# A post-norm transformer layer on one core: the first unit's row maxima sent in two halves

## The chip, the cores and the metric

The kernel runs on one core of one Trainium2 chip. TensorE (PE in the profile) multiplies, VectorE (DVE) and ScalarE (ACT) read and write PSUM and SBUF, GpSimd (POOL) works in SBUF, SyncE (SP) issues nearly all DMAs. The time is the device time of one execution in microseconds; lower is better.

## The reference

Input `x` is 4 batches of 1024 tokens with 128 features, all float32.

```
q, k, v = x @ w_q, x @ w_k, x @ w_v              # 16 heads of 64
logits  = q k^T / 8, causal mask, softmax over keys
x = layernorm(x + (probs @ v) @ w_o^T)
h = butterfly_up(x @ W_exp + b_exp)              # 512 wide, 9 stages
h = butterfly_down(gelu(h + up_bias))            # 9 stages
x = layernorm(x + h @ W_con + b_con + down_bias)
```

## The kernel before

Attention is cut into 32 units: one batch and one pair of heads each. A unit has 12 steps. A step is one block of 128 keys (`kt`) against one chunk of 512 queries (`qc`): steps 0 to 3 are chunk 0, steps 4 to 11 chunk 1; on a diagonal block only the part at or right of the diagonal is computed. For each of the two heads a step has two score matmuls into a PSUM bank `SC`: L692 (keys by the high part of the queries) and L696 (keys by the low part). The projections are split into a part rounded to float32r (`QH`, `KHL`'s high half, made by ScalarE, L797) and the remainder (`QL`, made by VectorE, L929). ScalarE then takes the exponential (L863), GpSimd masks (L504) and adds the blocks up (L519, L527, L528), and the value matmuls (L717, `pv`) follow several steps later.

The softmax needs a row maximum for each query. It is found ahead of the unit with matmuls of its own (L631, "max" work) into one of four PSUM banks `WORK`; VectorE reduces each to a column of `MP` (L991 with the causal mask, an instruction and its accumulator read, or L994 without it). A unit has 21 such groups, `MAXES`: the first 6 (`CHUNK0_MAXES`) concern the queries of chunk 0, the other 15 those of chunk 1. At the last one VectorE forms the negated maxima `NEGM` (L998), transposes them to `NROW` (four instructions, L1004), and SyncE sends them as one row into partition 64 of `QL` (`rows`, L408), where L696 adds them to the scores. L696 of a unit's first step waits for it (`m_landed`).

All 21 groups of the coming unit, its four projections (`("proj", n, c)`: n is 0 for queries and 1 for keys, c the chunk) and its value projections (`("v", i)`) are spread as "fillers" over the 12 steps of the running unit, by the table `FILL`: three places for each step, between the two heads, behind the second, and after the step's value matmuls. TensorE executes in this written order. Each filler takes the next `WORK` bank and waits until the fourth filler before it has been emptied (`take_work`); VectorE and ScalarE empty them in the same order. `("proj", 0, 0)` is made one unit further ahead than the rest.

Unit 0 has no unit in front of it, so its fillers stand in a list of their own, `PREFETCH`, executed before the first step: two query and two key projections, two value projections, all 21 max groups, and the first projection of unit 1. While it runs, SyncE works through a fixed queue: the weights, the copies of queries and keys to the other half of the partitions (`copies(0)`, L396 and L400), the loads of `w_o`, `W_con` and two bias rows, a small copy of the bias row (L429) which GpSimd awaits before its last two bias stages (L190 to L494), `W_exp`, the second batch of `x`, and then `rows(0)`. GpSimd executes in written order too: the bias stages come before the first mask of unit 0. VectorE also splits the weights for coming units (`stage_low`, `stage_v_low`, L929 with the outputs `WST` and `WSV`): these read two SBUF tensors, whereas its reads of `WORK` take one from PSUM.

After 32 units come the feed-forward part and the last normalisation.

Of the kernel before, what the change touches and what calls it, by code (L numbers as in the profile page):

```python
# [194 lines left out]
def post_norm_layer(nc, x, w_q, w_k, w_v, w_o, W_exp, b_exp, up_w, up_b, down_w, W_con, b_con, down_b, out):  # L195
    ctx = ExitStack()
    with ctx:
# [161 lines left out]
        def _(sp):  # L359
# [72 lines left out]
            rows(0)  # L432
# [144 lines left out]
        def _(pe):  # L577
# [105 lines left out]
            def scores(unit, s):  # L683
# [3 lines left out]
                for h in range(2):  # L687
# [6 lines left out]
                    if s == 0 and h == 0:  # L694
                        pe.wait_ge(m_landed, (unit + 1) * 16)
# [223 lines left out]
        def _(dve):  # L919
# [40 lines left out]
            def consume(u, f, at):  # L960
# [19 lines left out]
                elif f[0] == "max":  # L980
                    pieces = f[1]
# [206 lines left out]
```

## Time and profile before

| | us |
|---|---|
| median of 3 runs | 1035.09 |
| lowest, highest | 1034.93, 1035.8 |
| the profiled execution | 1035.9 |
| its span, first to last instruction | 1034.2 |
| TensorE busy | 1007.0 (97%) |
| VectorE busy | 778.0 (75%) |
| GpSimd busy | 750.9 (73%) |
| ScalarE busy | 613.1 (59%) |
| mean granted TensorE clock | 0.993 of full |

The span leaves out 1.7 us of the profiled execution that lie around it. Busy shares are means over the whole program; the change touches only the first 60 us or so, and there the timeline and the stretches tell more. The chain that ended last runs 92% over TensorE. In the first of 40 slices TensorE is busy 6 tenths, in the second 7, in the third 9; from there to the end 9 in every slice, down to the last (7). A row that joins several instructions ("x2") gives their common start and total.

### The profile page before, as it was taken

Reading aid. Unit: us, or ns where it says so; the run is one execution under the profiler, and the core shown is the slowest. Engines: PE = TensorE matmul, PEld = TensorE weight load, DVE = VectorE, ACT = ScalarE, POOL = GpSimd, SP = SyncE. Lnnn points to the kernel's source line nnn. Section 1 sums busy time; section 2 is a strip of 40 time slices with the busy share of each in tenths; the row PEclk is TensorE's granted clock in tenths of the full one; section 3 lists DMA queues with packets and bytes.
Section 4 is the critical chain, followed back from the end, with each engine's and each line's share of the span. In section 5 each row is a group of like instructions: output and inputs, shape, how many; then the busy total and the mean of one; then the engine's idle time right before and its main releaser. Section 6 shows DMA issues by size and latency. Waiting matters only on the chain.

```text
span 1034.2 us, 17742 instructions
## 1 busy us (share of the span) xinstructions
PE 1007.0 (97%) x5816; PEld 697.7 (67%) x5816; DVE 778.0 (75%) x2112; ACT 613.1 (59%) x1246; POOL 750.9 (73%) x715
## 2 busy tenths in 40 slices
PE   6799999999999999999999999999999999999997
PEld 4566676676666776676666766767666766765687
DVE  7767777877777777878788778877778888785356
ACT  3555656566656656666556656666555656665544
POOL 6567887777768887777778877777778887777510
PEclk8899999999999999999999999999999999999999
DMA  6233122233222222232232222332222222320002
GB/s 190 62 83 82 45 72 53 62 83 83 58 68 62 63 65 60 63 83 63 70 76 58 62 56 55 83 83 63 66 60 74 63 57 57 83 64 22 22 11 73
DMA packets 48602, 68.71 MB, mean 66 GB/s; under 512 B 15191, under 2 KB 25083, under 8 KB 48510
## 3 DMA queue, kind: packets, MB, share of 16 engines
q1 hardware_dynamic: 48510, 67.57, 25.3%
q8 instruction: 47, 0.77, 0.3%
q14 instruction: 45, 0.37, 0.1%
HBM read 31.11 MB, written 2.36 MB: 32 GB/s over the span
## 4 chain that ended last, share of the span: by engine, by line
PE 92%; DVE 3%; DMA 2%; ACT 1%; issue 1%; POOL 0%; SPq 0%; POOLq 0%; ACTq 0%
PE O L717 25%; PE WORK L631 14%; PE SC L692 14%; PE SC L696 13%; PE WORK L644 6%; PE WORK L679 3%; PE WORK L607 3%; PE WORK L609 3%; PE WORK L608 3%; PE WORK L772 2%; PE WORK L617 1%; PE WORK L619 1%; PE WORK L618 1%; DVE WORK L991 1%; DMA R<-RROW 1%
## 5 line engine op out<-in xcount | busy, mean ns | idle before, releaser
L863 ACT ACTIVATE PR<-SC 128x512 f32<-128x512 f32 (+3 forms) x768 | 352.3, 490 | 263.9 <-PE SC L696 231.4
L519 POOL TENSOR_TENSOR SUM<-SUM,PR 128x1024 f32<-128x1024 f32 (+3 forms) x256 | 419.0, 1637 | 14.8 <-POOL SUM L528 0.5
L991 DVE CUSTOM_DVE_ANT_0 WORK<-WORK,CMASK 128x128 f32<-128x128 f32 (+3 forms) x512 | 239.3, 514 | 65.7 <-PE WORK L631 65.6
L692 PE MATMUL SC<-QH,KHL 128*128 128x512 f32 (+3 forms) x768 | 268.8, 356 | 3.1 <-ACT PR L863 3.0
L696 PE MATMUL SC<-QL,KH 128*128 128x512 f32 (+3 forms) x768 | 261.7, 346 | 3.3 <-DMA QL<-NROW 3.3
L504 POOL TENSOR_SCALAR_AFFINE_SELECT PR<-PR 128x256 f32<-128x256 f32 x256 | 105.9, 415 | 198.0 <-ACT PR L863 197.9
L631 PE MATMUL WORK<-KHL,QH 128*128 128x512 f32 (+3 forms) x768 | 226.5, 365 | 5.9 <-DMA KH<-KHL 4.1
L717 PE MATMUL O<-PR,VLO 128*64 128x512 f32 (+3 forms) x1024 | 200.0, 522 | 0.3 <-DVE OT L1075 0.3
L692 PEld LDWEIGHTS SC<-QH,KHL 128*128 128x128 f32 x768 | 145.2, 189 | 60.7 <-ACT PR L863 28.5
L631 PEld LDWEIGHTS WORK<-KHL,QH 128*128 128x128 f32 x768 | 136.7, 191 | 59.3 <-issue 35.4
L994 DVE TENSOR_REDUCE MP<-WORK 128x1 f32<-128x512 f32 x256 | 164.1, 684 | 4.8
L696 PEld LDWEIGHTS SC<-QL,KH 128*128 128x128 f32 x768 | 145.4, 189 | 14.2 <-DMA QL<-NROW 3.7
L929 DVE TENSOR_TENSOR QL<-WORK,QH 64x512 fp32r<-64x512 f32 x128 | 88.0, 687 | 86.7 <-ACT QH L797 85.5
L528 POOL TENSOR_TENSOR SUM<-PR 128x768 f32<-128x768 f32 x64 | 135.9, 2124 | 1.4 <-ACT PR L863 1.4
L717 PEld LDWEIGHTS O<-PR,VLO 128*64 128x64 f32 x1024 | 64.9, 136 | 104.4 <-issue 77.0
L929 DVE TENSOR_TENSOR KHL<-WORK,KHL 64x512 fp32r<-64x512 f32 x128 | 88.1, 689 | 34.2 <-ACT KHL L797 32.1
L797 ACT ACTIVATE QH<-WORK 64x512 fp32r<-64x512 f32 (+1 forms) x132 | 78.0, 591 | 26.2 <-PE WORK L609 22.6
L797 ACT ACTIVATE KHL<-WORK 64x512 fp32r<-64x512 f32 x128 | 75.7, 592 | 5.0 <-PE WORK L609 1.4
L717 PE MATMUL O<-PR,VHI 128*64 128x256 f32 (+3 forms) x512 | 74.3, 432 | 0.0
L991 DVE DVE_READ_ACCUMULATOR2_ANT MP<- 128x1 f32 x512 | 72.3, 141 | 0.0
L717 PEld LDWEIGHTS O<-PR,VHI 128*64 128x64 f32 x512 | 36.8, 137 | 52.6 <-issue 46.6
L644 PE MATMUL WORK<-WOT,OT 128*128 128x128 f32 x512 | 63.8, 278 | 0.6 <-DVE OT L1075 0.6
(132 smaller groups left out, 1099.0 us busy)
## 6 DMA issues: line engine op xcount, KB each, us to landing
QH<-QH SPq DMA_DIRECT2D x128, 128.0 KB, 2.4
KH<-KHL SPq DMA_DIRECT2D x128, 128.0 KB, 2.3
R<-RROW SPq DMA_DIRECT2D x64, 256.0 KB, 3.8
SW<-in_L_ffn_up_weights_dram SPq DMA_DIRECT2D x9, 512.0 KB, 4.4
SW<-_L_ffn_down_weights_dram SPq DMA_DIRECT2D x9, 512.0 KB, 4.3
out_dram<-X SPq DMA_DIRECT2D x7, 256.0 KB, 2.3
X<-in_L_attn_x_BSE_dram SPq DMA_DIRECT2D x3, 512.0 KB, 4.5
X<-in_L_attn_x_BSE_dram SPq DMA_DIRECT2D x2, 256.0 KB, 3.3
```

Of the source, the lines that this page charges most:

```text
L519: nc.gpsimd.tensor_tensor(total, total, prob(unit, s), ALU.add).then_inc(add_done, 1)
L528: nc.gpsimd.tensor_tensor(total, first[:, :, START[s]:], prob(unit, s), ALU.add).then_inc(add_done, 1)
L631: t = nc.tensor.matmul(w[:, at_col:at_col + n], QH[:, nxt, h, qt * P:(qt + 1) * P], KHL[:, nxt, h, lo:lo + n], start=True, stop=True)
L644: t = nc.tensor.matmul(w[:, k * P:(k + 1) * P], attended(pair, qc)[:, k * P:(k + 1) * P], WOT[:, pair % PAIRS, :], start=pair < last, stop ...
L692: nc.tensor.matmul(dst, KHL[:, par, h, kt * P:(kt + 1) * P], QH[:, par, h, q0:q0 + n], start=True, stop=False)
L696: nc.tensor.matmul(dst, KH1[:, par, h, kt * P:(kt + 1) * P], QL[:, par, h, q0:q0 + n], start=False, stop=True).then_inc(scores_ready, 1)
L717: t = nc.tensor.matmul(O[qc][h * K:(h + 1) * K, START[s]:], values(unit, kt)[:, h * K:(h + 1) * K], p[:, h, :], start=kt == 0, stop=s == L ...
L797: return nc.scalar.activation(dst, src, ACT.Copy)
L863: nc.scalar.activation(prob(unit, s)[:, h, :], SC[use % NSC][:, 0:n], ACT.Exp, scale=K ** -0.5).then_inc(exp_done, 1)
L929: return nc.vector.tensor_tensor(dst, src, hi_part.bitcast(F32), ALU.subtract)
L991: op = nc.vector.tensor_tensor_reduce(cols, cols, CMASK[:, CH - n:], 1.0, LOWEST, ALU.add, ALU.max, cell)
L994: op = nc.vector.tensor_reduce(cell, cols, AX_X, ALU.max)
```

## The change

`PREFETCH` is cut shorter. The first key projection moves ahead of the first value projection; behind the four projections come only the 6 groups of chunk 0 and four more (`FIRST[6:10]`), then the second value projection, then the first projection of unit 1. VectorE forms `NROW` for the first time after the sixth group (chunk 1's columns still hold the initial value) and again after the last group. SyncE sends the maxima of chunk 0 with two DMAs of 4 rows, one for each head, directly behind `copies(0)` and so before `w_o`, and those of chunk 1 with two more, where `rows(0)` stood. L696 (L734 in the new file) waits in step 0 for the first two, and in step 4 for all four. The other 11 groups of unit 0, `("first", 10)` to `("first", 20)`, become fillers in steps 0 to 3 of unit 0. What stood there, the preparation of unit 1, moves: its projections from steps 0 and 1 to the end of step 3 and step 4, its value projections from steps 2 and 4 to 5 and 6, and its 21 max groups from steps 1 to 9 to steps 4 to 10. The split of unit 1's weights on VectorE goes behind the first `NROW`. Units 1 to 31 keep `FILL`.

```diff
+FIRST = [("first", i) for i in range(len(MAXES))]
...
+FIRST_FILL = [[[], [], []] for _ in range(NS)]
+FIRST_FILL[0] = [FIRST[10:11], FIRST[11:12], []]
...
+FIRST_FILL[3] = [FIRST[18:19], FIRST[19:21], [("proj", 1, 0), ("proj", 0, 1)]]
+FIRST_FILL[4] = [[("proj", 1, 1)], [], MAXES[0:1]]
...
+FIRST_FILL[10] = [MAXES[19:21], [("proj", 0, 0)], []]
...
-PREFETCH = [("proj", 0, 0), ("v", 0), ("proj", 1, 0), ("proj", 0, 1), ("v", 1), ("proj", 1, 1)] + MAXES + [("proj", 0, 0)]
+PREFETCH = [("proj", 0, 0), ("proj", 1, 0), ("v", 0), ("proj", 0, 1), ("proj", 1, 1)] + MAXES[:CHUNK0_MAXES]
+PREFETCH += FIRST[CHUNK0_MAXES:10] + [("v", 1), ("proj", 0, 0)]
...
+            def first_rows(c):
+
+                sp.wait_ge(nrow_made, c + 1)
+                for h in range(2):
+                    dst = QL[K:K + 1, 0, h, c * CH:(c + 1) * CH].rearrange("a (t c) -> a t c", t=TPC)
+                    row = h * TILES + c * TPC
+                    sp.dma_start(dst.bitcast(F32), NROW[row:row + TPC, :].bitcast(F32)).then_inc(m_landed, 16)
...
             copies(0)
             sp.sem_inc(sums_landed, 16)
+            first_rows(0)
             sp.dma_start(wo_nat, w_o.rearrange("e h k -> e (h k)")).then_inc(in_wo, 16)
...
-            rows(0)
+            first_rows(1)
...
+                    if f == ("first", CHUNK0_MAXES):
+                        evacuated(NUMBER[-1, ("proj", 0, 1)])
+                        evacuated(NUMBER[-1, ("proj", 1, 1)])
+                        pe.wait_ge(dup_landed[1], 64)
...
-                    if s == 0 and h == 0:
-                        pe.wait_ge(m_landed, (unit + 1) * 16)
+                    if (unit, s, h) == (0, 0, 0):
+                        pe.wait_ge(m_landed, 32)
+                    elif (s, h) == (0, 0) or (unit, s, h) == (0, FIRST_OF[1], 0):
+                        pe.wait_ge(m_landed, rows_landed(unit))
...
-                if f == LAST_PROJ:
+                if f == MAXES[CHUNK0_MAXES - 1]:
                     stage_low(1)
```

The order of instructions shows three places. TensorE first, where the work of step 3 ends and step 4 begins: L692 and L696 are scores, L631 a max group of unit 1. Before:

```order
L692 MATMUL SC<-QH,KHL 128x128 [waits exp_done]
L696 MATMUL SC<-QL,KH 128x128
L631 MATMUL WORK<-KHL,QH 128x384 [waits work_free3]
L631 MATMUL WORK<-KHL,QH 128x512 [waits work_free0]
L692 MATMUL SC<-QH,KHL 128x512 [waits exp_done]
L696 MATMUL SC<-QL,KH 128x512
L692 MATMUL SC<-QH,KHL 128x512 [waits exp_done]
```

and now (L728 and L734 are the scores, L667 a max group of unit 0 itself, L638 to L640 a projection of unit 1):

```order
L667 MATMUL WORK<-KHL,QH 128x512 [waits work_free2]
L667 MATMUL WORK<-KHL,QH 128x512 [waits work_free3]
L638 MATMUL WORK<-XTH,WST 128x512 [waits work_free0]
L639 MATMUL WORK<-XTH,WST 128x512
L640 MATMUL WORK<-XTL,WST 128x512
L638 MATMUL WORK<-XTH,WST 128x512 [waits work_free1]
L639 MATMUL WORK<-XTH,WST 128x512
L640 MATMUL WORK<-XTL,WST 128x512
L728 MATMUL SC<-QH,KHL 128x512 [waits exp_done]
L734 MATMUL SC<-QL,KH 128x512 [waits m_landed]
L638 MATMUL WORK<-XTH,WST 128x512 [waits work_free2]
```

A wait for rows stands in step 4 too, and the last key projection of unit 1, the third projection in these rows, stands behind it.

TensorE at the end of unit 0, from the last value matmul of step 9 (L717, now L755) over the bias work (L662, now L698) to step 10. Before:

```order
L717 MATMUL O<-PR,VLO 64x512
L662 MATMUL WORK<-ONES,R 128x1 [waits brow_made,work_free3]
L662 MATMUL WORK<-ONES,R 128x1 x3
L692 MATMUL SC<-QH,KHL 128x256 [waits exp_done]
L696 MATMUL SC<-QL,KH 128x256
```

and now:

```order
L755 MATMUL O<-PR,VLO 64x512
L698 MATMUL WORK<-ONES,R 128x1 [waits brow_made,work_free1]
L698 MATMUL WORK<-ONES,R 128x1 x3
L728 MATMUL SC<-QH,KHL 128x256 [waits exp_done]
L734 MATMUL SC<-QL,KH 128x256
L667 MATMUL WORK<-KHL,QH 128x512 [waits work_free2]
L667 MATMUL WORK<-KHL,QH 128x512 [waits work_free3]
```

The last two max groups of unit 1, which stood ahead of step 9's value matmuls, now stand behind them and in step 10.

SyncE between the copies and the first row, now (OT, R, BC and SW are the destinations of `w_o`, `W_con` and the bias rows; the copy of the bias row waits for `blocks_done`):

```order
L431 DMA QL<-NROW 1x4x128 [waits nrow_made]
L431 DMA QL<-NROW 1x4x128
L455 DMA OT<-in_L_attn_w_o_dram 128x1024
L456 DMA R<-in_L_ffn_W_con_dram 128x4x128
L457 DMA BC<-in_L_ffn_b_con_dram 128x128
L458 DMA SW<-in_L_ffn_down_bias_dram 128x128
L460 DMA R<-R 1x4x128 [waits blocks_done]
```

The first two rows are new there, and their wait for VectorE now stands before the loads and the copy for GpSimd.

## Rows read from the trace of the kernel before

**Rows 1.** Waits of TensorE over the whole span: total us, times, longest.

```profile
PE WORK L631 <- DMA KH<-KHL: 4.1, 2, 2.1
PE SC L696 <- DMA QL<-NROW: 3.3, 1, 3.3
```

**Rows 2.** Timeline, prefetch: start us, us, engine, line, operation, count [idle before].

```profile
10.17 0.63 PE L607 MATMUL WORK<-XTH,WST 128*128 128x512 f32 x1
...
11.69 1.20 ACT L797 ACTIVATE KHL<-WORK 64x512 fp32r<-64x512 f32 x2 [0.68 <-PE WORK L609]
...
12.10 0.39 PE L609 MATMUL WORK<-XTL,WST 128*128 128x512 f32 x1
...
15.84 1.39 DVE L929 TENSOR_TENSOR KHL<-WORK,KHL 64x512 fp32r<-64x512 f32 x2
...
17.26 0.68 DVE L929 TENSOR_TENSOR WST<-WQKV,WST 128x256 fp32r<-128x256 f32 x1
...
17.97 0.30 DVE L991 CUSTOM_DVE_ANT_0 WORK<-WORK,CMASK 128x128 f32<-128x128 f32 x1
...
21.52 0.14 DVE L991 DVE_READ_ACCUMULATOR2_ANT MP<- 128x1 f32 x1
```

**Rows 3.** Timeline, the end of the row maxima and the first score.

```profile
29.14 0.73 DVE L991 CUSTOM_DVE_ANT_0 WORK<-WORK,CMASK 128x512 f32<-128x512 f32 x1
...
31.05 0.56 SPq L408 DMA_DIRECT2D QL<-NROW  x1
...
32.91 0.80 PE L696 MATMUL SC<-QL,KH 128*128 128x512 f32 x1 [3.26 <-DMA QL<-NROW]
```

**Rows 4.** Timeline, GpSimd: the bias row's DMA, the work behind it, the first mask.

```profile
19.12 0.70 SPq L429 DMA_DIRECT2D R<-R  x1
...
22.29 2.28 POOL L192 TENSOR_TENSOR SUM<-R,SUM 1x512 f32<-1x512 f32 x2 [4.04 <-DMA R<-R]
...
35.36 0.41 POOL L504 TENSOR_SCALAR_AFFINE_SELECT PR<-PR 128x256 f32<-128x256 f32 x1 [4.38 <-ACT PR L863]
```

**Rows 5.** Groups by shape, 0 to 62 us: busy us, mean ns of one.

```profile
L994 DVE TENSOR_REDUCE MP<-WORK 128x1 f32<-128x512 f32 x16 | 10.1, 680 | 0.0
L519 POOL TENSOR_TENSOR SUM<-SUM,PR 128x1024 f32<-128x1024 f32 x3 | 7.1, 2376 | 0.5 <-POOL SUM L528 0.5
...
L929 DVE TENSOR_TENSOR QL<-WORK,QH 64x512 fp32r<-64x512 f32 x8 | 5.5, 688 | 2.4 <-ACT QH L797 2.2
```

**Rows 6.** Stretches: us, busy us of each engine (instructions), PEclk, DMA share, GB/s.

```profile
26.00:28.00 2.00, 2.00 (x5) 1.03 (x4) 2.00 (x7) 0.00 (x0) 1.99 (x2) 0.50 0.00 0
...
36.00:38.00 2.00, 1.94 (x10) 1.33 (x8) 0.88 (x2) 1.96 (x5) 0.00 (x0) 1.00 0.00 0
```

**Rows 7.** Timeline, unit 0, steps 3 to 5: maxima, weight split, GpSimd's sum.

```profile
41.91 0.30 DVE L991 CUSTOM_DVE_ANT_0 WORK<-WORK,CMASK 128x128 f32<-128x128 f32 x1
...
42.34 1.84 POOL L528 TENSOR_TENSOR SUM<-PR 128x768 f32<-128x768 f32 x1
...
42.51 1.96 DVE L929 TENSOR_TENSOR WST<-WQKV,WST 128x256 fp32r<-128x256 f32 x1
...
45.17 0.39 PE L617 MATMUL WORK<-WSV,XTH 128*128 128x256 f32 x1 [0.86 <-DVE MP L991]
...
47.81 0.41 DVE L929 TENSOR_TENSOR WSV<-WQKV,WSV 128x256 fp32r<-128x256 f32 x1
```

**Rows 8.** The split of WST over the whole span: min, median, max ns.

```profile
L929 DVE TENSOR_TENSOR WST<-WQKV,WST x32: 419/420/1957, 6.0 to 890.3; 128x256 fp32r<-128x256 f32 x32
```

**Rows 9.** Timeline, end of unit 0 and first scores of unit 1.

```profile
57.87 0.73 DVE L991 CUSTOM_DVE_ANT_0 WORK<-WORK,CMASK 128x512 f32<-128x512 f32 x1
...
60.35 0.38 PE L692 MATMUL SC<-QH,KHL 128*128 128x256 f32 x1
...
63.37 0.50 PE L692 MATMUL SC<-QH,KHL 128*128 128x512 f32 x1 [0.75 <-ACT PR L863]
...
63.70 0.39 PE L696 MATMUL SC<-QL,KH 128*128 128x512 f32 x1
```

More of the change, by code:

```diff
@@ L128 @@
 W1_SPLIT_AT = (UNITS - 1, 8)
+FIRST_FILL = [[[], [], []] for _ in range(NS)]
+FIRST_FILL[0] = [FIRST[10:11], FIRST[11:12], []]
+FIRST_FILL[1] = [FIRST[12:13], FIRST[13:15], []]
+FIRST_FILL[2] = [FIRST[15:16], FIRST[16:18], []]
+FIRST_FILL[3] = [FIRST[18:19], FIRST[19:21], [("proj", 1, 0), ("proj", 0, 1)]]
+FIRST_FILL[4] = [[("proj", 1, 1)], [], MAXES[0:1]]
+FIRST_FILL[5] = [[("v", 0)], MAXES[1:3], []]
+FIRST_FILL[6] = [MAXES[3:5], [], [("v", 1)] + MAXES[5:7]]
+FIRST_FILL[7] = [MAXES[7:9], [], MAXES[9:11]]
+FIRST_FILL[8] = [MAXES[11:13], [], MAXES[13:15]]
+FIRST_FILL[9] = [MAXES[15:17], MAXES[17:19], []]
+FIRST_FILL[10] = [MAXES[19:21], [("proj", 0, 0)], []]
+FIRST_FILLERS = [(s, place, f) for s in range(NS) for place in range(3) for f in FIRST_FILL[s][place]]
+assert sorted(f for _, _, f in FIRST_FILLERS if f[0] != "first") == sorted(f for _, _, f in FILLERS if f[0] != "norm")
 def unit_fillers(u):
@@ L134, in unit_fillers @@
     rows = []
-    for s, place, f in FILLERS:
+    for s, place, f in FILLERS if u > 0 else FIRST_FILLERS:
         if f[0] == "norm":
@@ L353, in prob, with rows_landed @@
             return PR[:, (unit * NS + s) % PRING, :, 0:n]
+        def rows_landed(unit):
+            return 64 + 16 * unit
         block = ctx.enter_context(nc.Block())
@@ L401, in copies @@
                             .then_inc(dup_landed[c], 16)
+            def first_rows(c):
[4 more added lines that the diff above has]
+                    sp.dma_start(dst.bitcast(F32), NROW[row:row + TPC, :].bitcast(F32)).then_inc(m_landed, 16)
             def rows(unit):
                 par = unit % 2
-                sp.wait_ge(nrow_made, (unit + 1))
+                sp.wait_ge(nrow_made, unit + 2)
                 dst = QL[K:K + 1, par, :, :].rearrange("a h (t c) -> a (h t) c", t=TILES)
@@ L446, in _ @@
             inverses(UNITS - 1)
-            sp.wait_ge(m_landed, 16 * UNITS)
+            sp.wait_ge(m_landed, rows_landed(UNITS - 1))
             for c in range(CHUNKS):
@@ L619, in filler @@
                         t = nc.tensor.matmul(out, XTL[:, lo:lo + P], WSV[:, 0, :], start=False, stop=True)
-                elif f[0] == "max":
-                    pieces = f[1]
-                    unit, nxt = u + 1, (u + 1) % 2
+                elif f[0] in ("max", "first"):
+                    pieces = f[1] if f[0] == "max" else MAXES[f[1]][1]
+                    unit = u + 1 if f[0] == "max" else 0
+                    nxt = unit % 2
+                    if f == ("first", CHUNK0_MAXES):
+                        evacuated(NUMBER[-1, ("proj", 0, 1)])
+                        evacuated(NUMBER[-1, ("proj", 1, 1)])
+                        pe.wait_ge(dup_landed[1], 64)
                     for c in range(CHUNKS):
@@ L823, in evacuate @@
                 w, free = WORK[at % NWORK], work_free[at % NWORK]
-                if f[0] in ("max", "out", "w2", "wo", "con", "bias"):
+                if f[0] in ("max", "first", "out", "w2", "wo", "con", "bias"):
                     return
@@ L979, in consume @@
                     op.then_inc(free, 1)
-                elif f[0] == "max":
-                    pieces = f[1]
+                elif f[0] in ("max", "first"):
+                    pieces = f[1] if f[0] == "max" else MAXES[f[1]][1]
                     dve.wait_ge(work_ready, at + 1)
@@ L995, in consume @@
                     op.then_inc(free, 1)
-                    if f == MAXES[-1]:
+                    if f == MAXES[-1] or (u < 0 and f == MAXES[CHUNK0_MAXES - 1]) or f == ("first", len(MAXES) - 1):
+                        made = 0 if u < 0 else 1 if f[0] == "first" else u + 2
                         dve.wait_ge(free, at // NWORK + 1)
```

8 lines of the change are left out of this document (5 added, 3 removed).

## The prediction

> **What bounds the kernel now.** I read the busy line and the slices first: TensorE is busy 97% of the span and from the third slice on nearly without a break, so what the prologue loses, TensorE loses for good, and a start earlier by a microsecond is worth at most a microsecond. Then the waits of TensorE: only two long ones are the prologue's, 3.3 us for the row of maxima and 2.0 of the 4.1 us for a copy of keys [rows 1]. Then the timeline up to the first scores of unit 1. It shows VectorE as the engine that paces the start. Two key conversions at 15.84 and the weight split run straight into the max groups at 17.97 [rows 2], and these into the last at 29.14, behind it NEGM and the transposes [rows 3]. TensorE meanwhile runs at half clock and only fills banks (26 to 28 us: granted clock 0.50, VectorE busy 2.00 of 2.00) [rows 6]. The last max group of unit 0 starts on VectorE at 29.14, the DMA of the row is issued at 31.05 (1.91 later), TensorE's L696 goes on at 32.91 (1.86 after that) [rows 3]. I use these two lags, 1.91 and 1.86, for every row below.
>
> So the question is not how early the first score comes, but how early VectorE and TensorE are done with all of unit 0's fillers: 21 max groups of unit 0 and 21 of unit 1, of which none is removed.
>
> **The head start.** The key projection of chunk 0 starts at 10.17 behind six value matmuls; it now starts about 1.3 earlier, at 8.9. ScalarE's conversion of it starts 10.4 instead of 11.69, then a value tile (0.60); the query projection of chunk 1 ends where it did, about 12.5 (its last matmul starts at 12.10), so queries 12.5 to 13.7, keys to 14.9 (1.20 each pair) [rows 2]. VectorE follows with two pairs of 0.69 each [rows 5] from 13.7 and is free at 16.5, before 17.23. The weight split (0.68) no longer stands next, so the max groups start at 16.5 instead of 17.97: 1.45 us gained, with no cost. Chunk 0's six groups take 21.52 - 17.97 = 3.55 [rows 2], to 20.05; the row DMA goes at 21.3. Two DMAs of 0.56 issue each instead of one: landed at 23.8.
>
> VectorE then does the weight split (0.42, to 21.8), one pair (about 0.5) and three reductions at 0.68 or a little under [rows 5], to 24.35. TensorE's second value projection needs the bank of that pair, free at 22.5; it and the projection behind it are six matmuls of 256 columns and three of 512, 2.6 us at 1.2 GHz (the clock of 0.50 in rows 6; 512 columns are 0.43 us): 25.15. The scores of step 0 start there, their rows having landed; L696 done at 26.0, against 33.7. This is the visible effect: 8 us.
>
> **What the steps 0 to 3 take back.** VectorE must next convert the query projection of unit 1, which ScalarE delivers (1.5 after the projection starts, then 1.20, as from 10.17 to 11.69 [rows 2]) at 26.55; VectorE waits 2.2 us for it, then 1.39: 27.95. Eleven groups stand behind it. Before, 21.52 to 29.14 were 7.6 us for the fourteen groups ahead of the last [rows 2, 3]; the first four are the 2.4 counted above, which leaves 5.2 for ten, and I add 0.3 where TensorE's matmul comes late: the last starts at 33.45. TensorE has less to do in these steps, so VectorE paces them. The DMA goes at 35.4, the second one 0.6 behind it, landed 37.85. The extra NEGM and transposes cost VectorE 1.1 us, counted above.
>
> Step 4's L696 (L734 now) waits for that row. TensorE has finished two projections at about 34.6 and stands still for 3.2 us: the wait of 3.3 us is not removed, it has moved. Behind it stands the last key projection. Before, the first matmul after such a pause took 0.80, against 0.39 for one of the same width at 12.10 [rows 2, 3]: half clock. So it runs 38.3 to 39.6; ScalarE converts it to 41.05, VectorE to 42.45. Only then can VectorE take the max groups of unit 1. In the kernel before that point was 41.91 [rows 7]. The 8 us are gone on VectorE: the same 21 groups start 0.5 us later.
>
> **From there to unit 1.** TensorE is ahead by what it can do without VectorE: at the second value projection (L617, 45.17 before [rows 7]) it will also have the scores of steps 5 and 6, eight matmuls at 0.23 apart, 1.84 us. VectorE before lost 1.5 us in the weight split of 1.96 instead of 0.42, which lay beside GpSimd's L528 from 42.34 [rows 7, 8]. The collision with that split is probably gone, which hangs on GpSimd. Its bias copy was issued at 19.12 with its work resuming at 22.29, and the first mask ran at 35.36 [rows 4]. SyncE now reaches the copy at 24.6 (21.3, two rows 1.2, the four loads 2.07 as before), so GpSimd resumes at 27.75 and ends the bias at 36.4: first mask 1.1 later than before, unit 0's first four masks and sums done by 42.2; the next sum starts when step 5's exponentials are done, at 43.9. The split at 43.2 to 43.6 fits between. L617 then comes at 44.4, 0.8 earlier.
>
> But GpSimd now gets its long sums (2.38 each [rows 5]) back to back from 43.9: 43.9 to 46.3 and 46.3 to 48.65. The second split, WSV, ran at 47.81 in 0.41 with GpSimd idle [rows 7]; it now falls at 47.2, into the second sum, and by the one case in rows 7 (it ended 0.3 after GpSimd's operation) it ends at about 49.0: 1.4 lost. From L617 to step 10 was 60.35 - 45.17 = 15.18 [rows 7, 9]; without the eight scores done earlier and the two max groups that now come later (0.46) it is 12.9, so 57.3, or 57.5 with small waits. The banks of step 8's max groups come free 1.4 to 1.8 later than TensorE could use them, at 50.3; it waits about 1.5: step 10 starts at 59.0 instead of 60.35.
>
> The Trainium skill's page "GPSIMD Engine Reference", section "8. Key points", says that GpSimd shares its SBUF interfaces with VectorE and contends with VectorE's instructions in a two-port mode or with two SBUF inputs. By that rule the collision is to be expected, and this trace agrees (1.96 us beside a GpSimd sum, median 0.42 [rows 7, 8]); without it the result would be rival 1.
>
> **The row of unit 1.** Before, its last max group started on VectorE at 57.87, so it landed at 61.6, and the first L696 of unit 1 ran at 63.70, 3.35 after step 10's start: 2.1 us of slack [rows 9]. Now the last two groups stand in step 10: from step 10's start 0.24 for the first head, 1.15 until VectorE starts the last, 1.91 and 1.86: 5.15 us, where 3.35 is needed. TensorE's lead of 1.35 us at step 10 shrinks by 5.15 - 3.35 = 1.8: L696 (L734 now) at 59.0 + 5.15 = 64.1, against 63.70. All later units are the same in both and TensorE-bound, so the difference goes to the end one to one.
>
> **Sum.** 0.4 us slower: span 1034.6 against 1034.2. The profiled execution (1035.9) lies 0.8 above the median of 1035.09, so I put the change on the median: **1035.5 us**, no change that can be measured. A difference under 0.2%, 2.07 us, is about what a measurement of this kernel cannot tell from none.
>
> **Unknown prices.** The clock in the first 25 us: if the nine matmuls at 22.5 run at full clock (0.39 at 12.10 against 0.63 at 10.17 [rows 2]), all up to 42.45 comes 1.1 earlier; the split of WST then touches a GpSimd sum and WSV falls deeper into one; I get 58.3 for step 10 and 0.25 us faster. A collision costs between 0 and the whole of a sum, 2.38; I take 1.4, by the times above.
>
> **Rivals.**
> 1. *No collision.* WSV falls on a gap of GpSimd. Step 10 starts at 57.5, the row of unit 1 still comes late: 57.5 + 5.15 = 62.65, 1.05 faster: 1034.0; with the early clock 1033.0. For it: the median split is 0.42 over 32 of them [rows 8]. Against: GpSimd's sums stand back to back. Chance 0.20.
> 2. *The head start is kept.* The wait for the second row turns out short because VectorE gets through its eleven groups earlier, and the row of unit 1 is in time. Then the 3.3 us wait [rows 1] is saved: 1031.8. For it: no group of unit 1 needs VectorE before its own projection is there, and VectorE's work alone would fit into less time. Against: the two new waits (for ScalarE at 24.35, for the late key projection) leave nearly as many. Chance 0.16.
> 3. *The clock stays low, slower.* Now TensorE pauses in step 4 (3.2 us) and in step 8, and between them has short pieces. Before, it was at clock 0.50 from 26 to 28 us although busy in all of it, with VectorE pacing it, and at full clock from 36 to 38 [rows 6]. If it is still at half clock until 47 us, its 6.5 us of work from 37.85 to the second value projection take 8.9, and that projection itself 0.6 more: 3.0 us later, 1038.5. It decides from the point where matmuls of 512 columns start 0.43 apart after 44 us. Chance 0.12.
> 4. My forecast, from 0.25 faster to 1.4 slower (a whole sum of GpSimd in the way), 0.4 slower as worked out: chance 0.52; its own range 1034.8 to 1036.5.
>
> The range that leaves out less than 2 in 10 takes in rival 1 and parts of 2 and 3: 1032.7 to 1037.6. Faster by over 0.2%: rival 2, 0.16, and 0.02 of rival 1 with everything early: 0.18. Slower: rival 3 and 0.02 of mine, 0.14. Same 0.68.
>
> **What would show it.** In the timeline after: first L734 finished near 26; a wait of about 3 us of TensorE for `QL<-NROW` in step 4, at 34.6 to 37.9, and a second of over 1 us at unit 1's first step near 64; the first max group of unit 1 on VectorE near 42.4; the WSV split over 1 us long, beside a GpSimd sum. The forecast is wrong if the wait at step 4 is under 2 us, if the first max group of unit 1 comes before 41, or if unit 1's first L734 starts before 61.6 or after 65.8.

## The result, and the profile after

| us | before | after |
|---|---|---|
| median (7 runs each) | 1035.38 | 1039.06 |
| lowest, highest | 1034.93, 1036.07 | 1037.85, 1040.16 |
| profiled execution, its span | 1035.9, 1034.2 | 1040.16, 1038.4 |

The ratio is 1.0034, interval 1.0023 to 1.0045: 3.7 us slower, which can be measured. Forecast were 1035.5 and no change.

Waits of TensorE over the whole span after (columns as in [rows 1]):

```profile
PE SC L734 <- DMA QL<-NROW: 4.7, 2, 3.4
PE WORK L667 <- DMA KH<-KHL: 4.1, 2, 3.6
...
PE WORK L667 <- DVE MP L1032: 1.9, 2, 1.6
```

The one wait of 3.3 us for a row [rows 1] has become two, 3.4 and 1.3 us, and a wait for VectorE's reductions (L1032) is new. The timeline after, prefetch and step 0:

```profile
16.60 1.05 PE L667 MATMUL WORK<-KHL,QH 128*128 128x128 f32 x6 [3.62 <-DMA KH<-KHL]
...
17.10 0.30 DVE L1029 CUSTOM_DVE_ANT_0 WORK<-WORK,CMASK 128x128 f32<-128x128 f32 x1 [0.81 <-PE WORK L667]
...
21.92 1.33 SPq L431 DMA_DIRECT2D QL<-NROW  x2
...
23.01 0.55 PE L648 MATMUL WORK<-WSV,XTH 128*128 128x256 f32 x1 [1.37 <-DVE MP L1029]
...
26.14 0.63 PE L734 MATMUL SC<-QL,KH 128*128 128x512 f32 x1
...
27.17 1.39 DVE L967 TENSOR_TENSOR QL<-WORK,QH 64x512 fp32r<-64x512 f32 x2 [2.57 <-ACT QH L835]
```

The first L734 runs at 26.14 where the first L696 ran at 32.91 [rows 3]. Then steps 3 to 6:

```profile
35.95 1.21 SPq L431 DMA_DIRECT2D QL<-NROW  x2
...
38.23 0.62 PE L734 MATMUL SC<-QL,KH 128*128 128x512 f32 x1 [3.38 <-DMA QL<-NROW]
38.42 1.24 SPq L422 DMA_DIRECT2D KH<-KHL  x2
...
41.52 0.76 PE L667 MATMUL WORK<-KHL,QH 128*128 128x128 f32 x2 [0.53 <-DMA KH<-KHL]
...
42.82 0.30 DVE L1029 CUSTOM_DVE_ANT_0 WORK<-WORK,CMASK 128x128 f32<-128x128 f32 x1
...
44.21 0.63 PE L728 MATMUL SC<-QH,KHL 128*128 128x512 f32 x1
...
44.64 0.63 PE L734 MATMUL SC<-QL,KH 128*128 128x512 f32 x1
...
45.61 0.30 DVE L1029 CUSTOM_DVE_ANT_0 WORK<-WORK,CMASK 128x128 f32<-128x128 f32 x1 [1.28 <-PE WORK L667]
...
46.92 0.28 PE L648 MATMUL WORK<-WSV,XTH 128*128 128x256 f32 x1
```

The pause of 3.38 us stands where it was forecast, and VectorE starts unit 1's maxima at 42.82 (before 41.91 [rows 7]). But at 45.61 VectorE has waited 1.28 us for TensorE, which reaches the second value projection at 46.92 (before 45.17 [rows 7]). The stretches show why (columns as in [rows 6], PEclk third from the end):

```profile
38.00:40.00 2.00, 1.76 (x5) 1.37 (x6) 0.76 (x2) 0.60 (x1) 2.00 (x4) 0.62 0.72 166
40.00:42.00 2.00, 1.48 (x5) 0.79 (x4) 0.60 (x1) 1.77 (x4) 2.00 (x3) 0.50 0.90 207
42.00:44.00 2.00, 2.00 (x9) 1.81 (x9) 1.96 (x7) 1.03 (x2) 2.00 (x3) 0.50 0.74 169
44.00:46.00 2.00, 2.00 (x9) 1.76 (x9) 0.72 (x4) 1.19 (x2) 0.80 (x3) 0.68 0.81 223
46.00:48.00 2.00, 2.00 (x14) 1.77 (x14) 2.00 (x8) 1.36 (x3) 2.00 (x1) 1.00 0.10 29
```

Behind the pause the granted clock is 0.50, the lower level of 1.2 GHz, until after 44 us (the scores at 44.21 and 44.64 still take 0.63 each), though TensorE is busy most of the time. So from 42.82 on it is VectorE that waits for TensorE, where the prediction had TensorE ahead of VectorE. The end of unit 0:

```profile
48.87 2.38 POOL L550 TENSOR_TENSOR SUM<-SUM,PR 128x1024 f32<-128x1024 f32 x1 [0.50 <-POOL SUM L559]
...
49.19 2.35 DVE L967 TENSOR_TENSOR WSV<-WQKV,WSV 128x256 fp32r<-128x256 f32 x1
...
52.20 0.38 PE L667 MATMUL WORK<-KHL,QH 128*128 128x256 f32 x1 [1.64 <-DVE MP L1032]
...
62.22 0.38 PE L728 MATMUL SC<-QH,KHL 128*128 128x256 f32 x1
...
65.63 0.57 SPq L438 DMA_DIRECT2D QL<-NROW  x1
...
67.50 0.50 PE L734 MATMUL SC<-QL,KH 128*128 128x512 f32 x1 [1.30 <-DMA QL<-NROW]
```

The WSV split takes 2.35 us, not 0.41 [rows 7], beside a sum of GpSimd, and TensorE pauses again (1.64). Step 10 starts at 62.22, 1.87 later than before; L734 of unit 1 waits for its row and runs at 67.50, 3.80 later than the 63.70 of [rows 9]. The span is 4.2 us longer; the remaining 0.4 arises later and was not traced. This profile is of the slowest of the seven runs (1040.16): the copy of keys that the first group awaits landed late (16.60), and all that follows is up to 0.8 us later than in the second profile of the same kernel, below.

### The profile page after: what moved, and what is told of

The parts are those of the page before. It is cut to its first block, busy times and chain, and to the rows that moved or that the text cites. A ratio compares the mean times of both kernels' runs of the same rounds, so it can differ in the third digit from the quotient of the medians.

```text
span 1038.4 us, 17751 instructions
## 1 busy us (share of the span) xinstructions
PE 1007.9 (97%) x5816; PEld 699.1 (67%) x5816; DVE 779.0 (75%) x2117; ACT 614.0 (59%) x1246; POOL 750.5 (72%) x715
## 4 chain that ended last, share of the span: by engine, by line
PE 90%; DMA 3%; DVE 3%; ACT 1%; issue 1%; SPq 1%; POOL 1%; POOLq 0%; ACTq 0%; DVEq 0%
PE O L755 25%; PE WORK L667 14%; PE SC L728 13%; PE SC L734 12%; PE WORK L680 5%; PE WORK L715 3%; PE WORK L638 3%; PE WORK L639 3%; PE WORK L640 3%; PE WORK L810 2%; PE WORK L648 1%; PE WORK L650 1%; PE WORK L649 1%; DMA R<-RROW 1%; DVE WORK L1029 1%
## 5 line engine op out<-in xcount | busy, mean ns | idle before, releaser
L728 PE MATMUL SC<-QH,KHL 128*128 128x512 f32 (+3 forms) x768 | 269.8, 357 | 3.1 <-ACT PR L901 3.1
L734 PE MATMUL SC<-QL,KH 128*128 128x512 f32 (+3 forms) x768 | 262.6, 347 | 4.7 <-DMA QL<-NROW 4.7
L667 PE MATMUL WORK<-KHL,QH 128*128 128x512 f32 (+3 forms) x768 | 225.1, 362 | 6.3 <-DMA KH<-KHL 4.1
L755 PE MATMUL O<-PR,VLO 128*64 128x512 f32 (+3 forms) x1024 | 200.0, 522 | 1.2 <-DVE OT L1116 1.2
L728 PEld LDWEIGHTS SC<-QH,KHL 128*128 128x128 f32 x768 | 145.8, 190 | 60.9 <-ACT PR L901 28.5
L667 PEld LDWEIGHTS WORK<-KHL,QH 128*128 128x128 f32 x768 | 136.0, 190 | 58.3 <-issue 35.7
L1032 DVE TENSOR_REDUCE MP<-WORK 128x1 f32<-128x512 f32 x256 | 164.1, 682 | 6.5 <-PE WORK L667 1.7
L734 PEld LDWEIGHTS SC<-QL,KH 128*128 128x128 f32 x768 | 145.9, 190 | 16.0 <-DMA QL<-NROW 5.4
L755 PEld LDWEIGHTS O<-PR,VLO 128*64 128x64 f32 x1024 | 64.9, 136 | 105.2 <-issue 77.7
L755 PE MATMUL O<-PR,VHI 128*64 128x256 f32 (+3 forms) x512 | 74.4, 432 | 0.0
L755 PEld LDWEIGHTS O<-PR,VHI 128*64 128x64 f32 x512 | 36.8, 137 | 52.6 <-issue 46.6
```

Source lines behind the costliest of these rows:

```text
L667: t = nc.tensor.matmul(w[:, at_col:at_col + n], QH[:, nxt, h, qt * P:(qt + 1) * P], KHL[:, nxt, h, lo:lo + n], start=True, stop=True)
L728: nc.tensor.matmul(dst, KHL[:, par, h, kt * P:(kt + 1) * P], QH[:, par, h, q0:q0 + n], start=True, stop=False)
L734: nc.tensor.matmul(dst, KH1[:, par, h, kt * P:(kt + 1) * P], QL[:, par, h, q0:q0 + n], start=False, stop=True).then_inc(scores_ready, 1)
L755: t = nc.tensor.matmul(O[qc][h * K:(h + 1) * K, START[s]:], values(unit, kt)[:, h * K:(h + 1) * K], p[:, h, :], start=kt == 0, stop=s == L ...
L1032: op = nc.vector.tensor_reduce(cell, cols, AX_X, ALU.max)
```

## The experiments

The theory after the result has three parts: the low clock behind the pause in step 4, the WSV split beside GpSimd's sum, and unit 1's row made late by the two groups behind the value matmuls. Each kernel starts from the changed one unless said otherwise. Where an edit adds lines, the line numbers in its profile move: L734, the scores with the low part of the queries, is L739 in e3 and e6, L742 in e8 and L747 in e9 and e11; in the text it keeps the name L734. "The filling" is the 12 extra matmuls of e3, e6, e9 and e11.

| kernel | median (range; runs) | before | ratio, interval |
|---|---|---|---|
| changed, again | 1039.03 (1037.73 to 1039.77; 5) | 1035.69 | 1.0033, 1.0020 to 1.0045 |
| e1 last groups | 1037.68 (1035.75 to 1039.70; 11) | 1035.56 | 1.0021, 1.0012 to 1.0029 |
| e2 split later | 1036.01 (1034.00 to 1038.56; 11) | 1035.56 | 1.0006, 0.9997 to 1.0014 |
| e3 warm | 1038.33 (1034.62 to 1039.90; 11) | 1035.56 | 1.0025, 1.0015 to 1.0034 |
| e4 key early | 1039.73 (1038.17 to 1041.35; 5) | 1035.56 | 1.0038, 1.0025 to 1.0050 |
| e5 rows behind | 1039.15 (1038.50 to 1039.71; 5) | 1035.69 | 1.0035, 1.0022 to 1.0047 |
| e6 split, warm | 1035.65 (1033.62 to 1037.69; 11) | 1035.69 | 0.9999, 0.9990 to 1.0007 |
| e7 prefetch only | 1034.51 (1032.90 to 1035.88; 11) | 1035.69 | 0.9989, 0.9980 to 0.9998 |
| e8 all | 1034.77 (1033.76 to 1035.58; 11) | 1035.83 | 0.9993, 0.9984 to 1.0002 |
| e9 all, warm | 1033.06 (1031.48 to 1033.94; 11) | 1035.83 | 0.9974, 0.9965 to 0.9983 |
| e10 prefetch, split | 1033.29 (1031.94 to 1036.27; 11) | 1035.83 | 0.9979, 0.9971 to 0.9988 |
| e11 both splits | 1032.30 (1031.79 to 1033.41; 6) | 1035.57 | 0.9966, 0.9954 to 0.9978 |

**The changed kernel again.**

> The changed kernel as it is, on the same chip as the three below, to see how far its own runs spread. Expected 1039.1 (1037.8 to 1040.2), 3.7 us over before.

The result repeats, 1039.03. In this execution the collision is 2.24 us, step 10 starts at 61.38 and L734 of unit 1 at 66.66: the same steps, each some 0.8 us earlier. The 0.8 us are there before step 4 already (VectorE's first max group 16.25 against 17.10, step 4's L734 37.38 against 38.23). Starting points of single profiles differ by that much, so below the distances between two steps count, not their times.

**e1: the last two groups ahead of step 9's value matmuls.**

```diff
-FIRST_FILL[9] = [MAXES[15:17], MAXES[17:19], []]
-FIRST_FILL[10] = [MAXES[19:21], [("proj", 0, 0)], []]
+FIRST_FILL[9] = [MAXES[15:17], MAXES[17:21], []]
+FIRST_FILL[10] = [[], [("proj", 0, 0)], []]
```

> The changed kernel with one line of its table altered: the last two max groups of unit 1 stand ahead of step 9's value matmuls again, as in the kernel before, and not in step 10. My theory: the row of unit 1 is late only because of these two; its first L734 then goes 3.35 us after step 10's start (as before) instead of 5.28, so at about 66.0 instead of 67.5, no wait for QL<-NROW in unit 1, time 1.4 to 1.9 us under the changed kernel (1037.2 to 1037.7). Rival: the row is not what holds unit 1 (ScalarE's last exponentials are), the wait only changes its name: 1039.1, within 0.4.

```profile
61.53 0.57 SPq L438 DMA_DIRECT2D QL<-NROW  x1
62.15 0.38 PE L728 MATMUL SC<-QH,KHL 128*128 128x256 f32 x1
...
65.50 0.39 PE L734 MATMUL SC<-QL,KH 128*128 128x512 f32 x1
```

Step 10 is where it was (62.15), the row leaves 4.10 us earlier, the wait is gone and L734 comes 3.35 behind step 10, as before the change. The distance from step 10 to L734 is 1.93 us shorter (3.35 against 5.28); the two groups now stand ahead of step 10 and cost TensorE about 0.5 there. That fits the 1.4 of the medians; their intervals overlap, so the mechanism rests on the profile.

**e2: the WSV split behind group 10, not group 6, in unit 0.**

```diff
-if f == MAXES[6] and u % 2 == 0 and u + 2 < UNITS:
+if f == MAXES[6 if u else 10] and u % 2 == 0 and u + 2 < UNITS:
```

> The changed kernel, with VectorE's split of WSV in unit 0 behind max group 10 instead of group 6, where GpSimd has no sum running (in the trace of the changed kernel it is idle from 51.3 to 54.4). My theory: the split takes 0.42 instead of 2.35, TensorE's 1.64 us wait in step 8 goes, step 10 starts 1.6 to 1.9 earlier (near 60.5), time 1037.2 to 1037.5. Rival: VectorE has slack behind step 8 (it waits 1.7 us for TensorE at 56.4), so what the collision costs is taken up there and the time stays within 0.5 of 1039.1.

```profile
49.18 0.41 DVE L967 TENSOR_TENSOR WSV<-WQKV,WSV 128x256 fp32r<-128x256 f32 x1
```

Faster by 3.0 us, more than expected: the split alone cannot give more than its 1.94 us. In this profile the clock came back at 40 to 42 us already (0.88 there, 1.00 from 42) and stayed, and step 10 starts at 57.63. Nothing in the edit acts before step 6, so the early return is chance. It shortened the way from step 4's L734 to the second value projection from 8.69 to 7.06 us; the edit shortened that from there to step 10 from 15.30 to 13.56. How many of the eleven runs had the early return is not known, so how the 3.0 us of the medians divide stays open.

**e3: TensorE kept busy in the first pause**, by 12 matmuls whose result nobody reads, ahead of step 4's wait.

```diff
+if unit == 0:
+    w = take_work(NUMBER[0, LAST_PROJ])
+    for _ in range(WARM_MATMULS):
+        nc.tensor.matmul(w[:, :], WST[:, 0, 1, :], XTH[:, 0:CH], start=True, stop=True)
```

> The changed kernel with 12 matmuls of 512 columns more: TensorE executes them in step 4 while it waits for the second row, into a bank that the next projection overwrites. Nothing else moves. My theory (the clock): granted clock 1.00 instead of 0.50 from 38 to 45.6 us, the key projection 0.6 us shorter, the second value projection at 44.6 to 45.2 instead of 46.92, unit 1's first L734 about 2 us earlier, time 1036.9 to 1037.4. Rival (VectorE and the copies set the pace): max group 0 waits for its copy of keys (41.5) and for VectorE as before, the clock is hidden, time within 0.6 of 1039.1.

The clock is 1.00 from 34 to 50 us. From step 4's L734 (37.04) to the second value projection (44.01) it is 6.97 us instead of 8.69. But then, first the stretches, then the timeline:

```profile
48.00:50.00 2.00, 0.38 (x1) 0.19 (x1) 2.00 (x4) 0.36 (x1) 0.48 (x1) 1.00 0.00 0
50.00:52.00 2.00, 1.99 (x7) 0.87 (x9) 1.94 (x6) 0.60 (x1) 0.33 (x1) 0.73 0.00 0
52.00:54.00 2.00, 2.00 (x8) 0.73 (x6) 0.00 (x0) 0.00 (x0) 2.00 (x2) 0.50 0.00 0
```

```profile
46.10 2.38 POOL L551 TENSOR_TENSOR SUM<-SUM,PR 128x1024 f32<-128x1024 f32 x1 [0.50 <-POOL SUM L560]
...
46.26 2.50 DVE L972 TENSOR_TENSOR WSV<-WQKV,WSV 128x256 fp32r<-128x256 f32 x1
...
49.42 0.38 PE L668 MATMUL WORK<-KHL,QH 128*128 128x256 f32 x1 [1.69 <-DVE MP L1037]
...
50.80 4.07 PE L760 MATMUL O<-PR,VLO 128*64 128x512 f32 x16
```

The second value projection comes 2.9 us earlier (1.2 of them from an earlier start of this execution, 1.7 from the clock) and its groups meet the same collision. Behind TensorE's pause of 1.69 us the clock falls a second time, and the 16 value matmuls of step 8 take 4.07 us, where they took 2.38 in the changed kernel: the 1.7 us won are lost again. In the medians 0.7 are left, which the intervals don't separate from nothing. In this execution the clock was paid twice; the changed kernel's own pause of 1.64 us at the same place did not bring it down.

**e4: the last key projection moved to the end of step 3.**

```diff
-FIRST_FILL[3] = [FIRST[18:19], FIRST[19:21], [("proj", 1, 0), ("proj", 0, 1)]]
-FIRST_FILL[4] = [[("proj", 1, 1)], [], MAXES[0:1]]
+FIRST_FILL[3] = [FIRST[18:19], FIRST[19:21], [("proj", 1, 0), ("proj", 0, 1), ("proj", 1, 1)]]
+FIRST_FILL[4] = [[], [], MAXES[0:1]]
```

> The changed kernel with the last key projection of unit 1 at the end of step 3, ahead of the wait for the second row, not behind it. Rival A (the one my prediction leant on: the late key projection sets VectorE's start of unit 1's groups): VectorE is done with that conversion 2.7 us earlier (40.1), the first group starts near 40.2 instead of 42.82, time 1036.5 to 1037. Theory B: the first group also needs the copy of keys that SyncE issues only behind the rows and two other copies (38.4, landed 41.5), so it gains 0.8 us at most on VectorE, and TensorE's clock stays at 0.50 behind the wait: 1038.3 to 1039.

```profile
35.49 1.21 SPq L431 DMA_DIRECT2D QL<-NROW  x2
...
37.96 1.23 SPq L422 DMA_DIRECT2D KH<-KHL  x2
...
41.06 0.77 PE L667 MATMUL WORK<-KHL,QH 128*128 128x128 f32 x2 [2.33 <-DMA KH<-KHL]
```

Not faster. TensorE's first group of unit 1 comes 5.57 us behind the row's DMA, exactly as in the changed kernel (35.95 to 41.52). What it waits for is the copy of keys, which SyncE issues behind the two rows (1.21) and the copies of queries (1.18). VectorE starts that group at 41.87, 6.38 behind the row instead of 6.87, where the conversion of the late projection (41.40 to 42.79) ended just ahead of 42.82. So the late key projection, to which my prediction put VectorE's start, costs 0.5 us; without it the copy sets nearly the same point. Neither shortens the time here: VectorE then waits 2.40 us for TensorE, which runs at 0.50 until 46 us.

**e5: the first rows sent where the second are, behind the loads.**

```diff
-            first_rows(0)
 ...
+            first_rows(0)
             first_rows(1)
```

> The changed kernel with the first half's row DMAs behind the weight loads instead of ahead of them; nothing else differs. My theory: the loads then leave at 17 us, GpSimd resumes its bias work near 22.5 instead of 30.5 and masks from 35 on, but unit 0's masks and sums had room to wait; what holds the later part (the second row, the copies, the split of WSV beside a GpSimd sum) is untouched, so the time stays within 0.6 of the changed kernel. Rival: sending the row ahead of the loads is what delays GpSimd and makes the collisions: 1037.5 or less, with the WSV split under 1 us.

1039.15, no difference that can be measured. The row itself leaves no later (21.45; the loads are issued by 20.0), so this tests only what the early wait does to GpSimd: it resumes at 21.50 instead of 30.52, and still the WSV split takes 1.85 us beside a sum. The rival, that the row ahead of the loads makes the collision, is out. In step 0 no wait for the row stands in either profile.

**e6: e2 and e3 together.**

> The changed kernel with both edits tried singly before: the WSV split behind max group 10, and 12 extra matmuls of 512 columns during the wait for the second row. Singly they gave 1036.0 and 1038.3, each with runs spread over 4.5 to 5.3 us. Theory (the clock falls after every TensorE pause of over about 1.5 to 3 us in this stretch, and the warm kernel lost in step 8, where its pause behind the WSV collision took the clock down again, what it had won in step 4): with both pauses filled or removed the clock stays at 1.00 from 30 us on, median 1035.0 to 1035.8, spread under 3 us. Rival (the clock costs nothing, the collision is all): 1036.0 as the split alone.

The clock is 1.00 from 34 to 54 us, the WSV split takes 0.41, step 10 starts at 57.35 and L734 at 62.64 with its wait of 1.3. With both pauses cured 3.4 us are back against the changed kernel (singly 0.7 and 3.0); against e2 the filling adds 0.4, inside the intervals. The distances are 6.98 and 13.02 us; the prediction had 6.5 and, without the collision, 12.9.

**e7: the kernel before, with one row and its own `FILL`, but the key projection first and the second value projection behind the maxima.**

```diff
-PREFETCH = [("proj", 0, 0), ("v", 0), ("proj", 1, 0), ("proj", 0, 1), ("v", 1), ("proj", 1, 1)] + MAXES + [("proj", 0, 0)]
+PREFETCH = [("proj", 0, 0), ("proj", 1, 0), ("v", 0), ("proj", 0, 1), ("proj", 1, 1)] + MAXES + [("v", 1), ("proj", 0, 0)]
-                if f == LAST_PROJ:
+                if f == MAXES[-1]:
                     stage_low(1)
```

> The kernel before, with only the prefetch put in another order: first key projection ahead of the first value projection, second value projection behind all 21 max groups, weight split of unit 1 behind the row. One row, sent where it was, FILL unchanged in unit 0. Theory: the head start on VectorE (1.45 us by my prediction, 0.9 to 2.0 in the traces so far) is kept whole, because nothing of unit 1 moves behind a new wait: first L696 of unit 0 at 31.2 to 32.0 instead of 32.91, time 0.9 to 1.5 us under before. Rival: the start is given back in unit 0 where VectorE and the copies set the pace: 1035.4, within 0.4.

```profile
28.72 0.57 SPq L408 DMA_DIRECT2D QL<-NROW  x1
...
40.19 1.83 POOL L528 TENSOR_TENSOR SUM<-PR 128x768 f32<-128x768 f32 x1
...
40.37 1.93 DVE L929 TENSOR_TENSOR WST<-WQKV,WST 128x256 fp32r<-128x256 f32 x1
...
43.00 0.39 PE L617 MATMUL WORK<-WSV,XTH 128*128 128x256 f32 x1 [0.84 <-DVE MP L991]
```

The row leaves 2.33 us earlier than at 31.05 [rows 3], and 2.17 of it reach the second value projection (45.17 [rows 7]). Faster by 1.2 us (the interval just leaves out no change): the VectorE time that the new order of the prefetch saves is worth something where nothing of unit 1 is moved.

**e8: e1, e2 and e4, and unit 1's first copies of queries ahead of the second rows.** The copies are taken out of `copies(1)` and put here:

```diff
+            query_copies(1, 0)
             first_rows(1)
```

> The changed kernel with four repairs of its table and queue: the last two max groups of unit 1 back in step 9, the WSV split behind group 10, the last key projection ahead of the wait for the second row, and SyncE's copies of unit 1's first queries ahead of the second row instead of behind it (so the copy of keys leaves 1.2 us earlier). Theory: max group 0 of unit 1 starts 4.9 us after the second row is issued instead of 6.9 on VectorE, unit 1's first L734 has no wait for its row; against the split alone (1036.0) 1 us less from the row and up to 0.8 from the copy: 1034.3 to 1035.0. Rival: the start of unit 0 in two halves gives back everything it gains, however the rest is placed: 1035.6 or more.

```profile
34.82 1.30 SPq L438 DMA_DIRECT2D QL<-NROW  x2
...
36.16 1.17 SPq L429 DMA_DIRECT2D KH<-KHL  x2
...
39.19 0.77 PE L675 MATMUL WORK<-KHL,QH 128*128 128x128 f32 x2 [0.34 <-DMA KH<-KHL]
```

```profile
40.00:42.00 2.00, 2.00 (x9) 1.81 (x9) 2.00 (x5) 0.60 (x1) 1.86 (x4) 0.50 0.70 154
```

The first group comes 4.37 us behind the row, 1.20 less than in e4, which is one pair of copies: SyncE's queue sets it. 4.3 us faster than the changed kernel, and 1.1 faster than the kernel before, with an interval that still takes in no change. The clock lies at 0.50 until 44 us, though TensorE is busy 2.00 of 2.00 in both stretches from 40 on. The WST split takes 1.53 us here.

**e9: e8 with 12 filling matmuls**, with keys and queries of unit 0 as operands, into the bank of unit 1's first group.

> The kernel with the four repairs, and 12 extra matmuls of 512 columns while TensorE waits for the second row (results overwritten). It shows what the clock is worth once the rest is mended. Theory: granted clock 1.00 from 30 us on, 0.5 to 1.2 us under the four repairs alone, 1033.5 to 1034.3. Rival: the extra matmuls only fill a pause, equal within 0.4.

```profile
40.32 2.35 DVE L980 TENSOR_TENSOR WST<-WQKV,WST 128x256 fp32r<-128x256 f32 x1
...
48.41 0.40 DVE L980 TENSOR_TENSOR WSV<-WQKV,WSV 128x256 fp32r<-128x256 f32 x1
```

The clock is 1.00 from 30 to 54 us, and the kernel 1.7 us faster than e8, with intervals that don't meet. From step 4's L734 to the second value projection it is 6.14 us instead of 7.85, also 1.7. That is the clock's price in this pair, which differs in nothing but the filling. The WST split collides here for 2.35 us instead of 1.53, so the price is rather above 1.7.

**e10: e7 with the WST split behind group 5 in unit 0.**

```diff
-if f == MAXES[0] and u + 2 < UNITS:
+if f == MAXES[0 if u else 5] and u + 2 < UNITS:
```

> The kernel before with the new order of the prefetch (tried singly: 1034.5, 1.2 under before), and in unit 0 VectorE's split of WST behind max group 5 instead of group 0, away from GpSimd's L528 beside which it took 1.93 us. Theory: the split takes 0.42 to 0.7, the second value projection's wait of 0.84 us for VectorE goes, another 0.8 to 1.2 us less: 1033.3 to 1033.8. Rival: TensorE is bound by its own work from there and by ScalarE, the pause moves to another place: 1034.5 within 0.4.

```profile
43.63 0.42 DVE L929 TENSOR_TENSOR WST<-WQKV,WST 128x256 fp32r<-128x256 f32 x1
...
44.42 0.51 DVE L929 TENSOR_TENSOR WSV<-WQKV,WSV 128x256 fp32r<-128x256 f32 x1
...
60.27 0.39 PE L696 MATMUL SC<-QL,KH 128*128 128x512 f32 x1
```

Both splits are short, and unit 1's first L696 runs at 60.27 instead of 63.70 [rows 9]. Two entries moved in the list and two splits placed anew bring 2.5 us, without halves of a row.

**e11: e9 with the WST split behind group 10.**

> The kernel with the four repairs and the extra matmuls, and in unit 0 the split of WST too behind max group 10, next to that of WSV; it took 2.35 us beside GpSimd's sums there (40.32 to 42.67). Theory: this was the last long collision on VectorE's path before the second value projection; it takes 0.42 now, and 1 to 1.9 us come off: 1031.2 to 1032.1. Rival: VectorE then waits for TensorE or for ScalarE instead, 1033.1 within 0.4, and the plain kernel with the new prefetch and one moved split (1033.3) is as good with fewer edits.

```profile
48.03 0.41 DVE L980 TENSOR_TENSOR WST<-WQKV,WST 128x256 fp32r<-128x256 f32 x1
48.36 0.42 DVE L980 TENSOR_TENSOR WSV<-WQKV,WSV 128x256 fp32r<-128x256 f32 x1
```

1032.30, 3.3 us faster than the kernel before and the lowest median here; against e9 it is 0.8, less than expected, and inside the intervals, as is the 1.0 against e10. In the profile only 0.37 reach step 10 (57.45 against 57.82).

## Why the prediction was wrong

The distances that the argument rests on, in us. A is from step 4's L734 to the second value projection, B from there to step 10, C from there to L734 of unit 1; the last column is the granted clock in the stretches 40 to 42 and 42 to 44.

| kernel | A | B | C | clock |
|---|---|---|---|---|
| foretold | 6.5 | 14.6 | 5.15 | |
| changed | 8.69 | 15.30 | 5.28 | 0.50, 0.50 |
| changed, again | 8.81 | 15.19 | 5.28 | 0.50, 0.50 |
| e2 split later | 7.06 | 13.56 | 5.28 | 0.88, 1.00 |
| e3 warm | 6.97 | 17.13 | 5.28 | 1.00, 1.00 |
| e6 split, warm | 6.98 | 13.02 | 5.29 | 1.00, 1.00 |

The steps in their order:

- *Head start on VectorE: right.* Foretold for 16.5, VectorE's first group started at 17.10 in the first profile, where the copy of keys landed late, at 16.25 in the second and at 16.63 in e5.
- *Step 0 earlier, and the gain given back on VectorE: right.* L734 of step 0 ran at 26.14 (foretold done at 26.0, so 0.8 late, and 6.8 us earlier than before, not 8), the second row's wait 3.38 (3.2), the pause's end 38.23 (37.85), VectorE's first max group of unit 1 42.82 (42.45).
- *GpSimd: wrong, without effect.* I had it resume the bias work at 27.75 and mask at 36.5; it resumed at 30.52, 5.2 us behind the issue of its copy instead of 3.2, and masked at 39.20. So the WST split did not fit between the sums and took 0.91 us, not 0.42. VectorE waited for TensorE right behind it (1.28), which hid that.
- *"From there to unit 1", the work from the row to the second value projection (A): this step failed.* I took 6.5 us (37.85 to 44.4), with the clock low for the last key projection alone and TensorE ahead of VectorE from there. It took 8.69 (38.23 to 46.92), 8.81 in the second profile: the clock stayed at 0.50 for some 7 us behind the pause, and VectorE waited for TensorE. Rival 3 had 8.9, and its test holds: L728 at 44.21 and L734 at 44.64 start 0.43 apart. It held in part only, since the clock was back before the value projection itself, which rival 3 had 0.6 us later still. I gave it 0.12; against it stood the kernel before, where the clock was back at 36 us, about 3 us behind the first score [rows 3, 6]. e3 and e6 show the term itself: with the clock at 1.00 the same way takes 6.97 and 6.98, so 1.7 to 1.8 of the 2.2 us are the clock, and the other 0.4 to 0.5 were missing from my sum at full clock too. e9 against e8 prices the clock at 1.7 us in the time.
- *The collision (B): right in kind, too small.* 1.94 us were lost, not 1.4, because the split fell at the start of a sum and not in its middle. TensorE's step 8 waited 1.64 and 0.21, against 1.5 foretold. B was 0.7 longer than foretold, and 13.02 in e6, where the collision is gone (12.9 foretold without it).
- *The row of unit 1 (C): right.* 5.28 instead of 5.15, a wait of 1.30; e1 takes 1.93 us of it away in the profile.
- *Sum.* L734 of unit 1 was foretold for 64.1 and ran at 67.50, past the 65.8 that I had named as the sign of being wrong. Of the 3.4 us 2.5 stand at the second value projection (46.92 against 44.4: 0.4 the later row, 2.2 the slower work behind it), 0.7 between it and step 10, 0.1 behind it. In the second profile it ran at 66.66, and of 2.6 us again 2.3 are A. The small loss that the sum ended with (0.4) was the difference of larger gains and losses, and its sign is no merit.

Why the clock came back late is open. It lay at 0.50 from 40 to 44 us in six profiles with a pause of 2.7 to 3.4 us there (changed, again, e1, e4, e5, e8) and was back at 40 to 42 in one, e2, which is the changed kernel up to there. The gap of 0.53 us for the copy of keys and the short pieces behind the pause do not explain it: e8 has a gap of only 0.34, is fully busy from 40 us on, and its clock stays low nearly as long.

The experiments also say what I had not weighed: the terms don't add. The filling is worth 0.7 us on the changed kernel, 0.4 on e2 and 1.7 on e8; on the changed kernel a second fall of the clock took it back in the profile, for e2 the early return of the clock without it can be the reason, which was not tested. e2's 3.0 us are more than its own split. The sum by separate terms is therefore itself a weak point.

No run shows a gain from the halves by themselves. Of what the change brought, the reordered prefetch is worth 1.2 us alone (e7) and 2.5 with its split moved (e10). With halves, all repairs and no filling (e8) the kernel is 1.5 us slower than e10, with intervals that barely overlap; with both splits moved and the filling (e11) it is 1.0 faster, which the intervals don't separate. Halves with both splits moved but without the filling, and e10 with the filling, were not run.

## What to carry to other kernels

An earlier start is worth what the bottleneck engine can finish with it: count when its last input is ready, not its first. A wait that is moved into the middle of TensorE's work must be priced with what the pause does to TensorE's clock in the work behind it; here that was 1.7 us. Matmuls that fill the pause can buy it back (1.7 us in e9), or the next pause takes it again (e3). Before moving VectorE's work that reads two SBUF operands, look at what GpSimd runs at the new place; one list index decided between 0.41 and 2.35 us.

## What the runs showed of the hardware

The price of the collision is a wait until a sum of GpSimd has ended, not a slower rate. VectorE's split of 128x256 (0.40 to 0.43 alone) took 2.35, 2.50 and 1.93 us, and each time ended 0.28 or 0.29 us behind the end of the GpSimd sum beside it (51.25 and 51.54 after the change, 48.48 and 48.76 in e3, 42.02 and 42.30 in e7). The short collisions fit too (0.51 us in e10, 0.84 for WST in e3). So the price is what is left of the sum when the split begins, and it can be more than one sum: in e9 the WST split began at 40.32 beside a sum that ended at 40.77, did not get through before the next, and ended at 42.67, again 0.29 behind that one:

```profile
41.10 1.28 POOL L559 TENSOR_TENSOR SUM<-SUM,PR 128x512 f32<-128x512 f32 x1
```

The Trainium skill's page "GPSIMD Engine Reference", section "8. Key points", says that the two contend when VectorE reads two SBUF inputs; these traces agree, with that price.

The granted clock fell to 0.50 behind pauses of TensorE of 3.38 us and, in e3, of 1.69, but not behind the 1.64 of the changed kernel (1.00 in every stretch from 52 to 62 us), nor behind 2.12 us in the kernel before (1.00 in every stretch from 36 to 62):

```profile
40.06 0.47 PE L631 MATMUL WORK<-KHL,QH 128*128 128x128 f32 x2 [2.12 <-DMA KH<-KHL]
```

So among pauses of 1.6 to 2.1 us the length alone did not decide. The Trainium skill's page "TensorE: Matmul & The Clock Gate", section "Part 1: The HAM clock gate (the "warmup" mystery)", says that the clock follows how busy TensorE has been lately and that the moment of its changes varies from run to run. The traces agree: 0.50 and 0.88 in the same stretch of alike kernels. The spread of the times doesn't follow the pauses: over 11 runs each it is 5.3 us in e3 and 4.6 in e2, but also 4.1 in e6 and 4.3 in e10, and only 1.8 in e8, whose clock is low until 44 us. Its cause is open. The expectation of e6 makes the clock's fall a matter of the pause's length; by the 1.64 and 2.12 above that does not come out of the traces.
